# A windowed-attention stage on one core: the scores of a step ahead of the weighted sums of v in TensorE's order

## What is computed

```python
h = _layernorm(xw, ln1_g, ln1_b)                     # windows of 8x8 tokens, 192 channels
qkv = (h @ qkv_w).reshape(-1, N, 3, nh, hd)          # 8 heads of 24
q, k, v = (qkv[:, :, 0], qkv[:, :, 1], qkv[:, :, 2])
attn = jax.nn.softmax(jnp.einsum('bnhd,bmhd->bhnm', q, k) * scale, axis=-1)
o = jnp.einsum('bhnm,bmhd->bnhd', attn, v).reshape(-1, N, C)
a = o @ proj_w + proj_b + xw
```

## Time and profile before

| | us |
|---|---|
| time, median of 3 runs | 3383.09 (3379.74 to 3383.64) |
| the profiled execution, its own time | 3377.27 |
| its span, first to last instruction | 3375.3 |
| the attention stage within it | 0 to 868 |

### The profile page before, as it was taken

How to read it: one execution, slowest core, us unless ns; L and a number is a source line. 1 busy time by engine, 2 the same in 40 slices (tenths; PEclk the granted TensorE clock), 3 DMA queues, 4 the chain that set the end, 5 groups by cost and what they waited for, 6 DMA issues and landing times. The chain is left out here.

```text
span 3375.3 us, 88476 instructions
## 1 busy us (share of the span) xinstructions
PE 3272.0 (97%) x31488; PEld 3202.0 (95%) x31488; DVE 2624.4 (78%) x6557; ACT 2015.6 (60%) x5417; POOL 1338.9 (40%) x2738
## 2 busy tenths in 40 slices
PE   8999999999899999999979979989999899999999
PEld 6899999999899999999979979989999899999999
DVE  5888888888477777767679989979999788875554
ACT  4788887888444444444447756669999555532222
POOL 5677777777333333333214300024444466630000
PEclk9999999999899999999989989999999999999999
DMA  2554444421144444444379866645555788877775
GB/s 70 125 159 151 151 151 152 132 60 41 27 135 142 126 150 123 146 129 135 119 208 297 272 200 198 200 122 161 170 162 168 221 234 234 235 232 229 227 225 169
DMA packets 473932, 555.81 MB, mean 165 GB/s; under 512 B 79446, under 2 KB 332828, under 8 KB 473500
## 3 DMA queue, kind: packets, MB, share of 16 engines
q1 hardware_dynamic: 447236, 530.68, 53.4%
q10 hardware_dynamic: 26264, 19.47, 1.8%
HBM read 404.55 MB, written 258.73 MB: 197 GB/s over the span
## 5 line engine op out<-in xcount | busy, mean ns | idle before, releaser
L1618 PE MATMUL PS<-dw_grid,dw_mats 128*128 128x196 f32 (+1 forms) x3840 | 625.4, 326 | 27.0 <-DVE dw_mats L1547 27.0
L1618 PEld LDWEIGHTS PS<-dw_grid,dw_mats 128*128 128x128 f32 x3840 | 624.5, 191 | 27.4 <-issue 27.4
L1427 PE MATMUL PS<-mlp_w,mlp_hid 128*128 128x192 f32 x2352 | 414.4, 326 | 0.5 <-ACT mlp_hid L926 0.5
L1543 DVE COPY dw_grid<-X 32x392 f32<-32x392 f32 (+1 forms) x480 | 290.2, 605 | 158.2 <-PE PS L1618 147.1
L1427 PEld LDWEIGHTS PS<-mlp_w,mlp_hid 128*128 128x128 f32 x2352 | 378.6, 190 | 0.8 <-ACT mlp_hid L926 0.8
L1973 PE MATMUL PS<-grn_gain,down_hi 128*128 128x384 f32 x1176 | 352.9, 361 | 10.9 <-POOL X_low L1926 10.9
L1259 POOL TENSOR_TENSOR X<-X,mlp_b 128x192 f32<-128x192 f32 x196 | 112.1, 590 | 535.2 <-DVE mlp_xn L875 535.1
L926 ACT ACTIVATE mlp_hid<-PS,mlp_b 128x256 f32<-128x256 f32 x588 | 247.2, 472 | 111.5 <-PE PS L917 111.5
L628 ACT ACTIVATE att_vbd<-PS,att_rs 64x96 f32<-64x96 f32 x784 | 263.9, 337 | 23.6 <-DVE att_rows L540 16.2
L1926 POOL TENSOR_TENSOR X_low<-X,down_hi 128x128 fp32r<-128x128 f32 x196 | 215.5, 1100 | 146.3 <-ACT down_hi L1936 146.3
L1585 ACT ACTIVATE dw_res<-PS,dw_brow 128x196 f32<-128x196 f32 x192 | 81.5, 424 | 295.6 <-PE PS L1618 295.6
(11 more groups left out here) (283 smaller groups left out, 10196.6 us busy)
## 6 DMA issues: line engine op xcount, KB each, us to landing
scratch_hid<-hid_hid SPq DMA_DIRECT2D x196, 320.0 KB, 3.3
down_hid<-scratch_hid SPq DMA_DIRECT2D x196, 320.0 KB, 3.7
scratch_wide<-scratch_taps SPq DMA_DIRECT2D x64, 960.0 KB, 6.5
dw_raw<-scratch_wide SPq DMA_DIRECT2D x96, 640.0 KB, 4.4
scratch_wide<-scratch_taps SPq DMA_DIRECT2D x64, 768.0 KB, 4.8
dw_raw<-scratch_wide SPq DMA_DIRECT2D x96, 512.0 KB, 3.8
scratch_u<-mlp_u SPq DMA_DIRECT2D x56, 378.0 KB, 3.8
att_x<-in_x SPq DMA_DIRECT2D x196, 96.0 KB, 3.5
```

The lines of the kernel that those rows point to most:

```text
L1427: last = nc.tensor.matmul(psD[i], hid[:, p.buf(2), m, i * 128:(i + 1) * 128], w2[:, m, :], start=(m == 0), stop=(m == MC - 1))
L1543: last = nc.vector.tensor_copy(dst, src)
L1618: last = nc.tensor.matmul(dst[:, :, ys, :], m, src, start=(i == 0), stop=(i == len(steps) - 1))
```

## The change

In TensorE's `body(t)` the block of lines that waits for and issues the weighted sums of v (L721) moves from ahead of the scores (L739) to behind them. No instruction, wait, size or buffer is added or taken away, and no other engine's code changes.

```diff
                     last.then_inc(q["proj"], 1)
-                b = t.back(AHEAD + 3)
-                if b.inside(NB):
-                    pe.wait_ge(q["pt_ready"], b.n + 1)
-                    pe.wait_ge(q["v_ready"], b.n + 1)
-                    pe.wait_ge(q["a_kept"], b.upto(4))
-                    if b.reached(1):
-                        pe.wait_ge(q["o_ready"], b.n)
-                    for hp in range(4):
-                        for w in range(2):
-                            last = nc.tensor.matmul(psPV[64 * w:64 * w + 64, hp * 50:hp * 50 + 50], pt[:, hp, 64 * w:64 * w + 64],
-                                                    vbd[:, b.buf(4), w, hp, :, :].rearrange("p e c -> p (e c)"), start=True, stop=True)
-                    last.then_inc(q["pv"], 1)
                 b = t.back(AHEAD + 1)
                 if b.inside(NB):
                     pe.wait_ge(q["qk_ready"], b.n + 1)
...
                     last.then_inc(q["scores"], 1)
+                b = t.back(AHEAD + 3)
+                if b.inside(NB):
+                    pe.wait_ge(q["pt_ready"], b.n + 1)
+                    pe.wait_ge(q["v_ready"], b.n + 1)
+                    pe.wait_ge(q["a_kept"], b.upto(4))
+                    if b.reached(1):
+                        pe.wait_ge(q["o_ready"], b.n)
+                    for hp in range(4):
+                        for w in range(2):
+                            last = nc.tensor.matmul(psPV[64 * w:64 * w + 64, hp * 50:hp * 50 + 50], pt[:, hp, 64 * w:64 * w + 64],
+                                                    vbd[:, b.buf(4), w, hp, :, :].rearrange("p e c -> p (e c)"), start=True, stop=True)
+                    last.then_inc(q["pv"], 1)
                 b = t.back(AHEAD)
```

## The result

| | us |
|---|---|
| before, median of 4 runs (the three above and one more) | 3382.62 (3379.74 to 3383.64) |
| after, median of 4 runs | 3498.53 (3497.07 to 3511.76) |
| after / before, 95% interval | 1.0353 (1.0327 to 1.0379) |
| the profiled execution of after: its time, its span | 3498.43, 3496.5 |

The account below looks back on a forecast made before the run. TensorE's own work list bounds the 4.14 us attention step. A stall of 0.56 plus 0.02 for late VectorE, in 192 steps, adds 111 us: 3488 on the profiled time, 3494 on the median; 3492 given, range 3466 to 3525.

Parts of the forecast that it names:

- Which wait is uncovered: TensorE's scores wait for the same step's residual add, until now covered by 0.60 us of weighted sums.
- The stall behind the slot: TensorE idle from the weighted sums' old start, 501.10, until the scores can start: 0.52 to 0.59 us per step.
- Both of my bounds: Latency from VectorE's end to TensorE's start: 0.05 us from L540, at most 0.12 from L551 to the scores.
- The step: Attention step between two residual adds: 4.66 to 4.73 us against 4.14 before.
- the seams: New TensorE orders, scores then weighted sums then L749: no difference taken, 0.03 us allowed either way.
- a late VectorE: VectorE gets the weighted sums later, so TensorE may wait for L577 or L567: 0.02 us per step taken.
- What is late next: VectorE's chain to L577's end takes 2.64 us; TensorE reaches the output transpose at 2.73, leaving 0.09 for latency.
- Rival A: VectorE's late chain becomes the bound with latency 0.22 us after L577: step 4.86, 3521 us; chance 0.09.
- The other wait of the chain: q/k/v wait for L567, ending at 1.32 us with TensorE there at 1.43: 0 to 0.01 us more.
- The early steps: Some 4 steps with VectorE late lose up to 0.5 us more, 2 us; about offset by existing idle time, left out.
- rival B: TensorE's clock swings from frequent stalls; a tenth of 192 steps at the lower level adds 54 us, 3546 us; chance 0.04.
- Rivals C and D: Semaphore index misread, so no stall: C gains at the seam behind the projection, 3363 us; D none, 3383; each 0.02.

Follow-up runs that it names:

- e3: Changed kernel with the transposes of the probabilities moved between projection and scores, weighted sums still behind the scores: 3505.47 us, 1.0373 of before.
- e6: Changed kernel with a second division of the weighted sums (184 of 192 columns, into a spare tile) ahead of L567: 3549.30 us, 1.0505 of before.
- e1: Changed kernel with the residual add no longer reading the projection (x plus x) and without the scores' wait for it: 3398.29 us, 1.0054 of before.
- e4: Kernel before, with a second add of the projection (184 columns, spare tile) ahead of the residual add: 3428.46 us, 1.0145 of before.
- e5: Changed kernel with a second add of the projection (184 columns, spare tile) ahead of the residual add: 3556.62 us, 1.0527 of before.

## Why the prediction was right

**Which wait is uncovered.** As forecast. The add's end to the scores was put between 0.05 and 0.12 us; it is 502.19 - (501.72 + 0.36) = 0.11, and 0.11 again where VectorE frees q/k/v in `e3` and `e6`. The stall behind the slot is 0.58, forecast 0.52 to 0.59. Both of my bounds came from rows, and the one from the same wait was right, while that of L540 was too short. `e1` showed the cause by taking it away, `e4` and `e5` by making it longer.

**The step.** Forecast 4.66 to 4.73 and 0.02 for VectorE, measured 4.75: 0.36 for the add, 0.11 to the scores, 0.45 for the scores (0.43 expected; after the stall their weight loads take 0.38 us, not 0.36), 0.61 for the weighted sums (0.60), 3.22 for the rest (3.22). The forecast took the middle of the latency and no difference at the seams, and both were at the upper end of what I allowed: 0.02 and 0.03 us. The 0.02 for a late VectorE were not needed and took back as much, which is luck. That leaves 0.03 us per step, 6 us in all. The whole adds up on the two profiled executions: 111 us forecast, 6 for the larger step, 6.1 for what is left in the stage, mostly early steps (below), less 1.8 for the earlier first add, is 121, and the spans differ by 3496.5 - 3375.3 = 121.2. The medians differ by 5 less, because the profiled execution of before was that much under its median, and that of after was not. I had allowed for 2 of the 5 by giving 3492 and not 3494.

**What is late next.** The chain from the weighted sums to L577's end was put at 2.64 us and measures 504.60 + 0.69 - 502.64 = 2.65; TensorE reaches the output transpose at 505.38 - 502.64 = 2.74, forecast 2.73, so the room is 0.09 and no stall shows. Rival A, a latency of 0.22 there, is out: the transpose starts 0.09 after L577. The other wait of the chain is the nearer one. L567 ends at 503.61 + 0.36 = 503.97 and q/k/v start at 504.08, 0.11 later, which is the latency seen in the waits; they also start 504.08 - 503.25 = 0.83 after the first load of the transposes, as in the earlier trace rows, so nothing is lost yet and no room is left. The working had TensorE there at 1.43 against 1.32 and a latency, 0 to 0.01 us, and that is what it is. `e3` and `e6` make this wait the limit.

**The early steps.** This was the step of the working that failed, in size. I set the lengthening where VectorE is late, some 4 steps with up to 0.5 us, 2 us in all, against stalls that fall into idle time, and left both out. The four steps from 69.14 to 96.32 us take 27.2 us in the changed kernel, against 70.05 to 89.47, 19.4, before: 7.8 us more, of which 4 x 0.61 = 2.4 are the common stall. Of the 5.3 us over, three of the steps have 0.8 to 0.9 each, and the one in which the clock falls, which I had not counted, has 2.8. The 5.3 are most of the 6.1 that are left in the stage, but the rest is a balance: the last five steps between adds took 2.2 us more than the stall gives, the first 1.3 less, and others are off either way.

**The clock.** In the steady part rival B didn't come: idle times of 0.54 us in each of some 170 steps, from 140 to 960 us, left the granted clock at 1.00. By the Trainium skill (TensorE: Matmul & The Clock Gate, "A second HAM failure mode: psum-queue depth-cycling") frequent short idle times between groups can make the clock swing; this trace has them in every step for over 800 us, and its granted clock doesn't bear that out. Between 60 and 140 us, where the kernel before stays at 1.00, the clock fell twice. The first time is in the steps where VectorE is late, behind a single idle time of 2.57 us. The second is near 130 us, behind this one:

```profile
128.64 0.49 PE L727 MATMUL PS<-att_qk 24*64 24x64 f32 x32 [2.73 <-issue]
```

VectorE and ScalarE stood in this step too, until about 127.7 us, and GpSimd until 128.2. What held them is not known, so the second spell can't be put down to the residual add alone. Nor does the length of an idle time settle it. In `e5` the scores (L731) kept their 0.49 us behind 2.83 us of idle time, with the granted clock at 1.00 from 77 to 96 us, and behind the next one of 2.83 the clock fell (0.72 from 96 to 102 us):

```profile
84.42 0.49 PE L731 MATMUL PS<-att_qk 24*64 24x64 f32 x32 [2.83 <-DVE X L555]
```

The highest of the runs, 3511.76 us, is 13 us above the others at a mean granted clock of 0.981, theirs 0.983; it has no profile, so where it lost them stays open.

**Rivals C and D**, my reading of the semaphore's index, are out: the scores start 0.11 us behind L551 of the same step, and that is the add whose end the trace names.

## What to carry to other kernels

Before a block is moved in an engine's order, ask what it was covering: look at the waits of the block that takes its place, and find which of them are signalled from work that was issued just before. A round trip of that kind (matmul out, other engine's operation, semaphore back) has a price that can be read from rows, here 0.58 us, and it is paid in every step if nothing independent stands in between. Then follow the moved block's own consumers as well: `e3` filled about half of the gap and gained nothing, because the consumers of the moved block had become as late as the stall.

## What was not expected of the hardware

Eight of the small matmuls (128 x 64 weights, 50 columns) took 0.37 us from their first load to the next block's, sixteen take 0.60 to 0.61. If such a block costs a fixed part and the same for each matmul, an estimate from these two gives a fixed part of 0.13 to 0.14 us, and cutting a block in two costs that again. No other length was tried. From VectorE's end to TensorE's first weight load it was 0.11 us in three different waits (L551, and L567 in `e3` and L572 in `e6`), and behind L577 it can't have been more than the 0.09 that were there, where a long wait for L540 had shown 0.05 and that for L537 0.22; why these two differ was not tried.
